# Lag marks in PSUM, GpSimd's normalisation ahead of the mask, and the mask last on VectorE, in an attention and mixture-of-experts layer

## What is computed

```python
x = x + attention(layernorm(x), ctx, ctx)
x = x + moe(layernorm(x), gate_w, w_gate_up, w_down, shared_w_gate_up, shared_w_down)
```

```python
corr = ifft(fft(q) * conj(fft(k))).real          # along the 64 positions
w, idx = top_k(corr over the lags, 8)
w = softmax(w)
out[pos] = sum_i w[i] * v[min(idx[i] + pos, 63)]
```

## Time and profile before

| what | us |
|---|---|
| median of 3 runs | 509.97 |
| lowest, highest | 509.71, 510.17 |
| span of the profiled execution | 507.2 |
| attention in the span, about | 0 to 204 |
| TensorE busy in the span | 476.8 |
| VectorE busy in the span | 312.2 |
| ScalarE busy in the span | 222.7 |
| GpSimd busy in the span | 227.3 |

### The profile page before, as it was taken

One profiled execution on the slowest core, in us unless ns is written; L12 is line 12 of the kernel. 1 busy time (PEld: TensorE's weight loads), 2 busy tenths in 40 slices (PEclk: granted clock), 3 DMA queues, 4 the chain that ended last, 5 costly groups with the idle time before them and its releaser, 6 DMA issues.

```text
span 507.2 us, 8574 instructions
## 1 busy us (share of the span) xinstructions
PE 476.8 (94%) x2097; PEld 328.1 (65%) x2098; DVE 312.2 (62%) x972; ACT 222.7 (44%) x425; POOL 227.3 (45%) x384
## 2 busy tenths in 40 slices
PE   4789999999999999898899999999999999999997
PEld 2556556656655655356576667766667678888885
DVE  3799899999999863884133333333333566747643
ACT  4778888888888835200122222122221435022120
POOL 2356676676667544044333333333333026466520
PEclk9899999999999999999999999999999999999999
DMA  4416533424253031801435555455554314555622
GB/s 157 163 43 237 173 110 127 145 63 146 68 180 114 36 103 43 331 0 43 124 113 157 165 165 151 150 158 161 165 153 151 131 63 126 159 174 165 207 62 83
DMA packets 24923, 66.76 MB, mean 132 GB/s; under 512 B 3456, under 2 KB 3456, under 8 KB 23488
## 3 DMA queue, kind: packets, MB, share of 16 engines
q1 hardware_dynamic: 18576, 45.74, 25.0%
q0 software_dynamic: 6320, 20.71, 15.6%
HBM read 45.73 MB, written 20.71 MB: 131 GB/s over the span
## 4 chain that ended last, share of the span: by engine, by line
PE 62%; DVE 15%; POOL 8%; issue 8%; ACT 5%; DMA 1%; SPq 0%; DVEq 0%; POOLq 0%; ACTq 0%
PE bank L457 19%; PE bank L655 17%; PE bank L670 8%; PE bank L643 4%; DVE top_v L923 4%; POOL arena L1198 4%; PE bank L469 4%; POOL arena L1201 4%; PE bank L558 2%; DVE arena L928 2%; PE bank L567 2%; DVE stats L886 2%; DVE resid L911 2%; ACT arena L772 2%; ACT arena L771 2%
## 5 line engine op out<-in xcount | busy, mean ns | idle before, releaser
L655 PEld LDWEIGHTS bank<-wgu_sb,x2T 128*128 128x128 f32 x376 | 67.6, 189 | 41.0 <-issue 33.6
L655 PE MATMUL bank<-wgu_sb,x2T 128*128 x376 | 92.0, 388 | 2.1 <-ACT x2T L814 0.6
L814 ACT COPY x2T<-bank 128x512 f32<-128x512 f32 x47 | 27.5, 585 | 142.6 <-PE bank L643 142.6
L1251 POOL DMA_INDIRECT xg_sb<-x_rows,gidx x47 | 45.9, 976 | 98.0 <-PE bank L643 93.6
L1083 DVE COPY actT_both<-bank 128x128 f32<-128x128 f32 x47 | 13.7, 291 | 73.3 <-PE bank L664 73.3
L670 PE MATMUL bank<-arena,actT_both 128*128 x94 | 47.9, 593 | 0.0
L457 PE MATMUL bank<-act_lo 128*128 128x512 f32 x96 | 41.2, 538 | 6.7 <-DVE act_lo L965 6.7
L457 PE MATMUL bank<-tokens_hi,shgu_hi 128*128 128x512 f32 x92 | 36.2, 394 | 0.0
L457 PE MATMUL bank<-tokens_hi,shgu_lo 128*128 128x512 f32 x92 | 35.8, 389 | 0.0
L457 PE MATMUL bank<-tokens_lo,shgu_hi 128*128 128x512 f32 x92 | 35.8, 389 | 0.0
L457 PEld LDWEIGHTS bank<-act_lo 128*128 128x128 f32 x96 | 18.7, 197 | 22.8 <-issue 20.8
(11 more groups left out here) (153 smaller groups left out, 1077.7 us busy)
## 6 DMA issues: line engine op xcount, KB each, us to landing
y_rows<-x2T SPq DMA_DIRECT2D x47, 256.0 KB, 3.1
wgu_sb<-w_gu SPq DMA_DIRECT2D x8, 1024.0 KB, 5.3
resid<-x SPq DMA_DIRECT2D x16, 256.0 KB, 2.8
arena<-ctx SPq DMA_DIRECT2D x16, 256.0 KB, 3.3
x_rows<-arena SPq DMA_DIRECT2D x16, 256.0 KB, 2.1
result<-resid SPq DMA_DIRECT2D x16, 256.0 KB
arena<-w_down SPq DMA_DIRECT2D x1, 3072.0 KB, 13.0
shgu_sb<-sh_gu SPq DMA_DIRECT2D x1, 2048.0 KB, 8.0
```

The source lines that it names most:

```text
L655: last = mm(ps_gu[b][:, 0:2 * INTER], xgT[b][:, c * P:(c + 1) * P], wgu_sb[:, bass.ds(at + c * 2 * INTER, 2 * INTER)], start=c == 0, stop= ...
L814: copy(xgT[b], ps_xgT[:, :]).then_inc(xgT_ready, 1)
L1251: nc.gpsimd.indirect_dma_start(xg[b], None, x2_rows[:, :], bass.IndirectOffsetOnAxis(ap=gidx[b][:, 0:1], axis=0)).then_inc(gathered[b], 16)
```

## The change

The marks are written into `ps_corr` itself, in place of `lagw`, so that the correlation bank holds `TAKEN` at the eight lags. Marking therefore waits until L928 has read the bank (`centered`), and TensorE's next correlation waits for `lagw_ready`, the end of the mask, where it waited for `lags_marked`. The sum and the reciprocal move ahead of the even products. GpSimd normalises all of `expz` (not the masked weights) between its two steps of the odd product. The mask becomes VectorE's last step of the turn, behind the odd product, the moments and the next products; it reads the marks from PSUM and the normalised `expz`, and writes `lagw`, which TensorE transposes. The semaphore `masked` goes and `weights_normal` comes. In the turn of pair 0 the next products stand where they stood (ahead of the moments). The moments now precede the products in every turn.

```diff
@@ tensor: iteration
                     pe.wait_ge(products_ready, p + 1)
-                    wait(pe, lags_marked, p)
+                    wait(pe, lagw_ready, p)
@@ vector: iteration
                     tt(segs(expz), lags, largest.to_broadcast([P, SEGS, L]), ALU.subtract).then_inc(centered, 1)
-                    wait(dve, lagwT_psum, p)
+                    dve.wait_ge(centered, p + 1)
                     apart(dve, dve_passed)
                     for s in range(SEGS):
-                        last = nc.vector.match_replace(segs(lagw)[:, s], tops[:, s], lags[:, s], TAKEN)
+                        last = nc.vector.match_replace(lags[:, s], tops[:, s], lags[:, s], TAKEN)
                     last.then_inc(lags_marked, 1)
+                if live(n, 0):
+                    p, _ = pair(h, b, 0)
+                    dve.wait_ge(exp_ready, p + 1)
+                    nc.vector.reduce_sum(top_s[:, :], segs(top_e[:, :]), axis=AX.X).then_inc(top_sum_ready, 1)
+                    dve.wait_ge(top_sum_ready, p + 1)
+                    nc.vector.reciprocal(top_r[:, :], top_s[:, :]).then_inc(top_r_ready, 1)
                 if live(n, -1):
...
                 if n == 0:
                     products(h, b, n)
-                if live(n, 0):
-                    p, _ = pair(h, b, 0)
-                    dve.wait_ge(exp_ready, p + 1)
-                    nc.vector.reduce_sum(top_s[:, :], segs(top_e[:, :]), axis=AX.X).then_inc(top_sum_ready, 1)
-                    dve.wait_ge(lags_marked, p + 1)
-                    stt(lagw, lagw, TAKEN, expz, ALU.is_equal, ALU.mult).then_inc(masked, 1)
-                    dve.wait_ge(top_sum_ready, p + 1)
-                    nc.vector.reciprocal(top_r[:, :], top_s[:, :]).then_inc(top_r_ready, 1)
                 if live(n, -1):
...
                     tt(odd_prod, ps_w_odd[:, :], ctx_odd_re[pb], ALU.mult).then_inc(out_products_ready, 1)
-                if n == -1:
-                    moments_ahead(h, b, n)
+                moments_ahead(h, b, n)
                 if n != 0:
                     products(h, b, n)
-                if n != -1:
-                    moments_ahead(h, b, n)
+                if live(n, 0):
+                    p, _ = pair(h, b, 0)
+                    dve.wait_ge(weights_normal, p + 1)
+                    wait(dve, lagwT_psum, p)
+                    stt(lagw, ps_corr[:, :], TAKEN, expz, ALU.is_equal, ALU.mult).then_inc(lagw_ready, 1)
@@ gpsimd
+            def normal(h, b, n):
+                if live(n, 0):
+                    p, _ = pair(h, b, 0)
+                    pool.wait_ge(top_r_ready, p + 1)
+                    w = segs(expz)
+                    nc.gpsimd.tensor_tensor(w, w, top_r[:, :].unsqueeze(2).to_broadcast([P, SEGS, L]),
+                                            ALU.mult).then_inc(weights_normal, 1)
+
             def odd_product(h, b, n):
                 if live(n, -1):
                     p, pb = pair(h, b, -1)
                     pool.wait_ge(w_odd_sw_ready, p + 1)
                     nc.gpsimd.tensor_tensor(w_odd_sw, w_odd_sw, ctx_odd_im[pb], ALU.mult).then_inc(odd_im_products, 1)
+                normal(h, b, n)
+                if live(n, -1):
                     pool.wait_ge(out_products_ready, 2 * p + 2)
                     pool.wait_ge(odd_im_products, p + 1)
                     nc.gpsimd.tensor_tensor(odd_prod, odd_prod, w_odd_sw, ALU.add).then_inc(odd_product_ready, 1)
@@ gpsimd: iteration
                     keep(h, b, n)
-                    if n != PAIRS - 1:
-                        odd_product(h, b, n)
-                if live(n, 0):
-                    p, _ = pair(h, b, 0)
-                    pool.wait_ge(masked, p + 1)
-                    pool.wait_ge(top_r_ready, p + 1)
-                    w = segs(lagw)
-                    nc.gpsimd.tensor_tensor(w, w, top_r[:, :].unsqueeze(2).to_broadcast([P, SEGS, L]),
-                                            ALU.mult).then_inc(lagw_ready, 1)
-                if n == PAIRS - 1:
                     odd_product(h, b, n)
```

More of the change, by code:

```diff
@@ L312, in build @@
         maxima_ready, centered, lags_marked = sem("maxima_ready"), sem("centered"), sem("lags_marked")
-        exp_ready, top_sum_ready, masked = sem("exp_ready"), sem("top_sum_ready"), sem("masked")
+        exp_ready, top_sum_ready, weights_normal = sem("exp_ready"), sem("top_sum_ready"), sem("weights_normal")
         top_r_ready = sem("top_r_ready")
```

## The result

| | before | after |
|---|---|---|
| median, us | 509.84 (509.53 to 510.17) | 517.23 (516.9 to 518.05) |
| ratio, 95% interval | | 1.0147 (1.0124 to 1.017) |
| span of the profiled execution | 507.2 | 515.1 |
| first L923 (pair 0) | 13.95 | 13.51 |
| pair 0 to pair 1 | 8.62 | 10.72 |

The change costs 1.5%, 7.4 us. The forecast was 511.7, slower by 1.7, with a range that ended at 516.8. The lower part of the table, made from the rows of L923 in the timeline, says where the 7.9 us of the span went: 2.1 into the first turn, 6.0 into the 14 turns behind it, 0.2 behind the maxima of pair 15, and the start came 0.4 sooner. Every one of the 14 turns takes 11.52 or 11.53 us, where before nearly all took 11.07.

The account below looks back on a forecast made before the run. The bound was the loop of VectorE up to L953, L1201, L469 and corr, 11.08 us a turn. First turn +2.2, 13 turns -0.3, the end -0.25 and +0.1 gave +1.7: 511.7 us, range 508.7 to 516.8.

Parts of the forecast that it names:

- the products 1.21: VectorE's new order: the next products take 1.21 us directly after the aggregate, and the mask begins at 8.12.
- The first turn: Turn of pair 0: corr of pair 1 waits for the mask, 2.2 us later, once, at the low clock.
- the rival of a clock that is up in time: Corr of pair 1 at full clock: first turn costs 0.6 in place of 2.2, 510.1 us; chance 0.10.
- The last turns: Turn before pair 15 has no moments, so -0.25 us; pair 15 is masked later, +0.1.
- The new waits: VectorE's waits on L928 before marking (0.83 where 0.60 stood) and on the sum before the reciprocal (0.25).
- the two new waits cost nothing: Rival: VectorE's waits on L928 and the sum add no time, a turn falls to 10.83, 508.4 us; chance 0.13.
- Marks in PSUM: VectorE's eight marks written to PSUM cost nothing extra, 1.59 us; upper bound 0.7 us per turn.
- The rival that they are dearer: Marks in PSUM cost 0.35 us more per turn, 516.6 us, or 521.5 at the whole bound; chance 0.20.
- The mask's price: VectorE's mask with marks from PSUM and the other input from SBUF takes 0.68 us, against L946's 1.10.
- the rival of a slow mask: GpSimd holds up the mask even with a PSUM input, up to 0.42 more per turn, 517.2 us; chance 0.07.
- GpSimd's chain: GpSimd's L1198 step starts at 4.11, then the multiply, L1201 ends at 7.71; alone it closes a turn in 10.83.
- The sign: Whole kernel slower, by 1.7 us to 511.7; slower 0.62, same 0.21, faster 0.17.

Follow-up runs that it names:

- third buffer: Changed kernel with a third buffer for the even context spectrum, so ScalarE's copies wait for even products one pair older; 511.21 us, ratio 1.0017.
- the kernel with the mask ahead: Changed kernel with the mask ahead of the next products in place of behind them; 510.11 us, ratio 1.0004.
- the marks in SBUF: Changed kernel with marks back in SBUF and the correlation released by the marks, not the mask; 509.65 us, ratio 0.9984.
- the first of the better orders: Changed kernel with marks in SBUF, no wait for the centred lags, correlation released by marks, sum and reciprocal behind the even products; 506.45 us, ratio 0.9920.
- before, with the sum ahead: Kernel before with only the sum and reciprocal moved ahead of the even products; 510.16 us, ratio 0.9990.
- the two better orders: Changed kernel, marks in SBUF, no centred-lags wait, sum behind even products: 506.45 us; the same with sum behind odd product, GpSimd normalising last: 502.28 us.

## Why the prediction was wrong, point by point

**The step that failed** is one term of VectorE's new order: "the products 1.21" right behind the aggregate, with no wait. I put them at 6.91 us after L923. They start at 112.21 - 104.89 = 7.32, behind 0.44 of idle time in which VectorE waits for ScalarE's copies. I had followed what is queued behind VectorE's and GpSimd's moved steps, but for the even products, which the sum, the reciprocal and the wait for the centred lags push back, I did not look up who waits for their end. The cue stood in my own rows: L896 carries "0.15 <-ACT arena L732", so ScalarE's copies were already the later of L896's inputs, and a shift of VectorE to an earlier L896 was bounded by them. Corrected by the trace of after, 11.06 + 0.41 = 11.47, and the rest to 11.52 is a hand-over from VectorE to TensorE of 0.14 (113.42 + 0.68 = 114.10 to 114.24) where I took 0.06, less 0.03 in the correlation (2.17 to L923 against 2.20). Over 14 turns, 11.52 in place of the 11.09 of before makes 6.0 us; I had -0.3 for 13 of them and -0.25 for the last.

The third buffer shows that the other terms hold: without the copies' wait the turn is 11.02 (11.06 forecast), the last one 10.84 (10.83), the first 10.82 (8.62 + 2.2), and the median 511.21 (511.7), though by its own runs of the kernel before that is +0.8 and not +1.7.

**The first turn:** right. +2.2 was forecast, +2.10 came, and the rival of a clock that is up in time falls for this execution (0.50 from 21.00 to 22.00). Corr starts 20.55 - 13.51 = 7.04 after L923, 2.19 later than the 4.85 of before, at the low clock as assumed; from its start to L923 it takes 3.68 against 3.77.

**The last turns:** -0.25 was forecast, none came, for the reason above: without the moments L896 waits 1.37 in place of 0.44. Behind pair 15 the forecast was +0.1, and +0.2 came.

**The new waits:** right. L928 to the first mark is 0.83 (106.21 to 107.04), where 0.60 stood before, sum to reciprocal 0.25 (108.64 to 108.89). So the rival "the two new waits cost nothing" is wrong for this kernel. The sentence of the Trainium skill (VectorE: DVE Perf Modes, The DRAIN you can't avoid) that I set beside it does not carry over to these instructions.

**Marks in PSUM:** right to take nothing. Eight marks take 1.60 (107.04 to 108.64) against 1.59. The rival that they are dearer falls, although its price, 516.6, is near to what was measured.

**The mask's price:** right, 0.68 with one input from PSUM; the rival of a slow mask falls, although its price, 517.2, is what was measured, by chance. Either of two things makes it cheap: the input from PSUM (0.69 wholly beside GpSimd's wide L1211, in the kernel with the mask ahead) or the place (0.68 with two SBUF inputs and no wide operation beside it, with the marks in SBUF). L946's 1.10 had neither.

**GpSimd's chain:** right. L1206 starts at 4.10, L1211 ends at 7.62 (7.71 forecast), and it doesn't set the turn. In the first of the better orders it does, at 10.73, where I had worked out 10.83.

**The sign:** right, for the first turn alone; the size was off by a factor of four. Of my rivals none had ScalarE in it.

## What to carry to other kernels

When a step is moved, list not only what is queued behind it but everyone who waits for its end, the writers that wait for its buffer to come free among them; with two buffers such a wait reaches the producer of the next tile but one. A short wait in brackets on an instruction says which input is the next bound: an instruction that is to start earlier can do so only as far as that input does. No bracket does not mean no wait: compare the start with the end of each input. A delay that costs nothing in one order costs in full once the same instruction lies in the loop, so each wait has to be priced in the new order.

## What the runs showed of the hardware that I had not expected

VectorE marks in place in PSUM at the same pace as into SBUF (1.60 against 1.59 us for eight). The mask with two SBUF inputs takes 1.10 us beside a wide GpSimd operation (L946 beside L1198, kernel before), 0.91 where it starts in the last 0.36 us of one (before, with the sum ahead), and 0.68 with no wide operation beside it; in the first two it ends 0.54 and 0.55 behind the end of GpSimd's operation. With one input from PSUM it takes 0.69 even beside a wide one. It works the other way too: a one-column operation of GpSimd that starts during the mask with two SBUF inputs takes longer (L1187 0.67 in place of 0.19 with the marks in SBUF; L1184 1.07 and 0.88 in place of 0.55 in the two better orders), while beside the mask with a PSUM input L1186 takes its 0.19 (changed kernel).

The granted clock falls to 0.50, the lower level, in the first two turns in every profile, but not at the same place. In the kernel before (TensorE idle for 2.71) and in the changed kernel (4.93) the first correlation runs low, and the clock is back at 1.00 when L512 comes, which takes 1.12. With the mask ahead (4.93 idle) the low stretch begins while TensorE is still idle, before L481 at 21.05. With the marks in SBUF (3.29 idle) it reaches beyond L512, which takes 2.07, and the turn behind takes 12.07 us in place of 10.96. In the kernel before with the sum ahead (3.16 idle) the whole correlation runs at 1.00; the fall comes only behind a second idle time, and the turns take 7.50 and 12.63 where the kernel before has 8.62 and 11.06. The rows of the stretches, first with the mask ahead:

```profile
20.00:21.00 1.00, 0.00 (x0) 0.00 (x0) 0.76 (x2) 0.33 (x1) 0.52 (x3) 0.50 0.98 319
```

With the marks in SBUF, a stretch and L512:

```profile
26.00:27.00 1.00, 0.85 (x1) 0.50 (x2) 0.82 (x3) 0.28 (x3) 0.00 (x0) 0.50 0.02 8
...
26.15 2.07 PE L512 MATMUL bank<-arena,const_sb 128*128 128x512 f32 x2 [0.67 <-ACT arena L750]
```

In the kernel before with the sum ahead, the correlation and the fall behind it:

```profile
21.00:22.00 1.00, 1.00 (x12) 1.00 (x11) 0.76 (x2) 0.60 (x1) 0.94 (x1) 1.00 1.10 360
26.00:27.00 1.00, 1.00 (x4) 0.48 (x2) 0.96 (x9) 0.91 (x2) 0.00 (x0) 0.50 0.00 0
```

Each kernel was profiled once, so how much of this belongs to the kernel and how much to the execution is not shown. The turn of 12.07 says that where the low stretch falls can be worth about a microsecond; a difference of that size between two kernels is better read from the steady turns.
